# Attention denominators: a product with zeros and ones and one wide reciprocal in place of two block transpositions

## What is computed

```python
attn = softmax(scores, axis=-1)              # over the keys
ctx = einsum('bhqk,bhkd->bhqd', attn, v)     # [heads, tokens, 8]
ctx = ctx.transpose(0, 2, 1, 3).reshape(b, s, 128)
return ctx @ Wo
```

## Time and profile before

| | |
|---|---|
| median of 3 runs | 988.42 us (985.24 to 991.22) |
| the profiled execution's own time | 983.89 us |
| its span, first to last instruction | 982.1 us |
| mean granted TensorE clock | 0.953 of full speed |
| back stages | 32 (2 attentions, 16 items), first copy at 55.6 us, last at 838.8 us |

### The profile page before, as it was taken

The page is one execution under the profiler, slowest core; times in us unless marked ns, Lnnn a source line. Parts: engine busy times, 40 slices in busy tenths (PEclk is TensorE's granted clock), DMA queues, the critical chain, the costliest instruction groups (busy, mean ns, idle before and its releaser), DMA issues.

```text
span 982.1 us, 36375 instructions
## 1 busy us (share of the span) xinstructions
PE 846.8 (86%) x15235; PEld 514.6 (52%) x15235; DVE 641.8 (65%) x1566; ACT 557.4 (57%) x974; POOL 299.0 (30%) x387
## 2 busy tenths in 40 slices
PE   5888989889889988979887899798899789879895
PEld 3334435545444544545444545456465566757793
DVE  2547585976677566657767866568485566656773
ACT  3556747666485836745756566454558364425552
POOL 2432222222331322132223202325223343443452
PEclk9999999999799999979999899999999899989998
DMA  7998100000000000000000100001100011114633
GB/s 178 388 333 296 49 24 8 8 24 8 29 18 14 12 14 19 9 23 3 19 22 15 36 18 19 23 19 32 42 19 19 28 46 40 50 44 126 178 104 123
DMA packets 50190, 60.90 MB, mean 62 GB/s; under 512 B 5872, under 2 KB 36464, under 8 KB 49648
## 3 DMA queue, kind: packets, MB, share of 16 engines
q1 hardware_dynamic: 34768, 27.19, 9.6%
q10 hardware_dynamic: 10272, 21.14, 6.3%
q0 software_dynamic: 4992, 10.27, 3.1%
HBM read 22.92 MB, written 35.65 MB: 60 GB/s over the span
## 4 chain that ended last, share of the span: by engine, by line
PE 48%; DVE 27%; issue 11%; ACT 5%; POOL 4%; DMA 3%; another core or an unknown queue 1%; SPq 0%; POOLq 0%; DVEq 0%; ACTq 0%
DVE row_max L1336 13%; PE ps L927 9%; PE ps L787 6%; PE ps L754 5%; PE ps L1012 4%; PE ps L765 3%; POOL eo_rows L1640 2%; PE ps L801 2%; PE ps L810 2%; PE ps L1004 2%; PE ps L793 2%; PE ps L1006 2%; PE ps L1005 2%; ACT probs L1164 2%
## 5 line engine op out<-in xcount | busy, mean ns | idle before, releaser
L1336 DVE TENSOR_REDUCE row_max<-ps 128x4 f32<-128x1024 f32 (+1 forms) x256 | 267.7, 1078 | 109.6 <-PE ps L765 62.7
L1164 ACT ACTIVATE probs<-ps 128x1024 f32<-128x1024 f32 x128 | 130.1, 1029 | 77.8 <-PE ps L787 66.7
L754 PE MATMUL ps<-bias_t,ch 64*32 64x512 f16 x2048 | 112.1, 395 | 26.7 <-DVE row_max L1336 12.2
L1164 ACT ACTIVATE stage<-ps 128x1024 f32<-128x1024 f32 x96 | 96.9, 1025 | 60.1 <-remote 31.7
L1640 POOL DMA_INDIRECT eo_rows<-eo_t,to_t x92 | 89.4, 972 | 117.8 <-ACT eo_t L1216 97.0
L1604 POOL TENSOR_TENSOR ctx_sb<-ctx_raw,ctx_sb 128x512 f32<-128x512 f32 x32 | 40.7, 1272 | 172.6 <-DVE ctx_sb L1364 172.5
L927 PE MATMUL ps<-probs,v_pad 128*32 128x256 f32 x1024 | 85.4, 400 | 3.2 <-ACT probs L1164 2.0
L1004 PE MATMUL ps<-xT_t,wgu_hi 128*128 128x256 f16 x276 | 77.6, 281 | 8.8 <-issue 2.8
L1495 DVE SCALAR_TENSOR_TENSOR gate_s<-gate_t,ps 128x256 f32<-128x256 f32 x138 | 57.1, 414 | 40.5 <-ACT gate_t L1210 30.8
L1627 POOL DMA_INDIRECT slot_rows<-rows,slots x64 | 63.2, 987 | 66.1 <-DVE slots L1444 51.8
L1012 PE MATMUL ps<-wd,hid 128*128 x552 | 74.2, 287 | 9.9 <-ACT xT_t L1202 5.8
(11 more groups left out here) (168 smaller groups left out, 1596.1 us busy)
## 6 DMA issues: line engine op xcount, KB each, us to landing
slot_rows<-eo_g ACTq DMA_DIRECT2D x1, 12642.0 KB, 48.0
slot_rows<-eo_g ACTq DMA_DIRECT2D x1, 7998.0 KB, 26.1
x_t<-slot_rows SPq DMA_DIRECT2D x46, 129.0 KB
eo_g<-eo_rows SPq DMA_DIRECT2D x16, 256.0 KB
xT<-in_x SPq DMA_DIRECT2D x16, 128.0 KB
kept<-resid SPq DMA_DIRECT2D x16, 128.0 KB, 1.7
resid_b<-kept SPq DMA_DIRECT2D x16, 128.0 KB
out_dram<-outT SPq DMA_DIRECT2D x16, 128.0 KB
```

Of the source, the lines that this page charges most:

```text
L754: eng.matmul(ps[HR * c:HR * (c + 1), two[r], :].rearrange("p (j s) -> p j s", j=2), csth("flip")[half, :], bias_t[half, way, 2 * g:2 * g + ...
L1164: eng.activation(probs[a][:, 2 * (k % 2):2 * (k % 2) + 2, :], both_of("c%d" % a, i, "e%d" % k), ACT.Exp).then_inc(z["exp"], 1)
L1336: ins = eng.tensor_reduce(row_max[a][:, qt, 4 * g:4 * g + 4].rearrange("p (r j) -> p r j", r=2), of_heads, AX.X, ALU.max)
```

## The change

A 128x128 matrix of zeros and ones, `den`, joins the f32 constants (the late part of them, loaded to `cf` at L1672). Its column `m` has a single one, in the row that holds the denominator of the head to which row `m` belongs; rows 16 to 31 of a block, which hold no context, get a denominator as well. In place of the three VectorE steps, TensorE multiplies `den` with the whole of `ctx_raw` (one f32 product of 512 columns into a rotating bank, step `den`), so that every partition has its denominators in place, and VectorE takes one reciprocal of 128x512 from that bank to `ctx_sb` (step `rec`). The GpSimd product and the output product are as before. In the plan, `den` is given 0.85 us on TensorE and takes a bank, and `rec` 0.69 us on VectorE and gives it back. The wait for the late constants moves from the first `out` to the first `den`. The tiles `rden` and their two memsets go.

```diff
--- before.py
+++ after.py
@@ -41,7 +41,7 @@
 
 CF, CF_COLS = {}, 0
 for _n, _w in (("ident", P), ("centre", D), ("kmask", HJ), ("kones", HJ), ("expert", NX), ("tri", NX * NX), ("tile", T_MAX), ("eights", T_MAX),
-               ("first", len(PARTS) * NX), ("zero", 1), ("half", 1), ("own", 2), ("to", 2 * KT), ("cos", KT * HD), ("sin", KT * HD)):
+               ("first", len(PARTS) * NX), ("zero", 1), ("half", 1), ("own", 2), ("to", 2 * KT), ("cos", KT * HD), ("sin", KT * HD), ("den", P)):
     CF[_n] = (CF_COLS, CF_COLS + _w)
     CF_COLS += _w
 CH, CH_COLS = {}, 0
@@ -198,7 +198,7 @@
     def back(self, a, i, free):
         job = "b%d" % a
         last = self.op((job, i, "ctx"), "act", 0.60, [("c%d" % a, i, "end")] + self.before(job, i), (), X)
-        last = self.chain(job, i, last, ("byq", "dve", 0.62), ("rec", "dve", 0.35), ("byd", "dve", 0.62), ("ctxn", "pool", 1.3))
+        last = self.chain(job, i, last, ("den", "pe", 0.85, ONE), ("rec", "dve", 0.69, (), "mine"), ("ctxn", "pool", 1.3))
         return self.op((job, i, "out"), "pe", 0.88, [last] + free, ONE)
 
     def b1(self, i):
@@ -487,7 +487,7 @@
 
 
         q_rows, k_head, v_pad, probs = {}, {}, {}, {}
-        qk_tok, row_max, ctx_raw, ctx_sb, rden = {}, {}, {}, {}, {}
+        qk_tok, row_max, ctx_raw, ctx_sb = {}, {}, {}, {}
         for a in (1, 2):
             big = ("q_rows", 2 * NG * S, F16), ("k_head", 2 * NG * HJ * S, F16), \
                 ("v_pad", KT * H * HR, F32), ("probs", 4 * 2 * S, F32)
@@ -503,8 +503,6 @@
             row_max[a] = sb("row_max%d" % a, [P, KT, H])
             ctx_raw[a] = sb("ctx_raw%d" % a, [P, 2, S])
             ctx_sb[a] = sb("ctx_sb%d" % a, [P, 2, S])
-
-            rden[a] = sb("rden%d" % a, [P, KT * S // HR, 4])
         onehot = probs[1][0:NBUCKET, 0:2, :]
         by_parts = probs[1][0:H, 2:4, :].bitcast(F16).rearrange("h k (o f) -> h k o f", o=2)
 
@@ -630,7 +628,7 @@
                                                             ("r1", "sq var v root"), ("r2", "sq var v root spread n"))}
 
         att = {a: signals("a%d_" % a, "qk v hi again vz lo kspread qspread krow qrow score max "
-                          "mxhi mxlo maxt clear qmax wscore exp pv ctx byq rec byd ctxn o") for a in (1, 2)}
+                          "mxhi mxlo maxt clear qmax wscore exp pv ctx den rec ctxn o") for a in (1, 2)}
         x1_done, h2_done = sem("x1_done"), sem("h2_done")
         rot_done = signals("rot_", "cos sin sum")
         hand = signals("hand_", "tok hi lo to l step gap e hot both ahead rank slot resid")
@@ -684,6 +682,8 @@
                 return rot_done["sin"], i + 1
             if name == "out":
                 return (x1_done if job == "b1" else h2_done), i + 1
+            if name == "den":
+                return z["rec"], i + 1
             if name in ("centre", "turn"):
                 return norm["n" + job[1]]["n" if name == "centre" else "h"], i + 1
             return {"qk": z["lo"], "v": z["vz"], "c0": z["ctx"], 
@@ -932,10 +932,14 @@
 
         def pe_back(eng, a, i, at):
             job, z = "b%d" % a, att[a]
+            yield at("den")
+            bank = free_bank(eng, job, i, "den")
+            if a == 1 and i == 0:
+                eng.wait_ge(s_w2, 16 * N_W2)
+            eng.wait_ge(z["ctx"], i + 1)
+            eng.matmul(bank, cst("den"), ctx_raw[a][:, :, :].rearrange("p r s -> p (r s)"), start=True, stop=True).then_inc(z["den"], 1)
             yield at("out")
             bank = free_bank(eng, job, i, "out")
-            if a == 1 and i == 0:
-                eng.wait_ge(s_w2, 16 * N_W2)
             eng.wait_ge(z["ctxn"], i + 1)
             eng.matmul(bank[:, 0:S], W["o%da" % a], ctx_sb[a][:, 0, :], start=True, stop=False)
             eng.matmul(bank[:, 0:S], W["o%db" % a], ctx_sb[a][:, 1, :], start=False, stop=True).then_inc(z["o"], 1)
@@ -1350,20 +1354,11 @@
 
         def dve_back(eng, a, i, at):
             z, job = att[a], "b%d" % a
-            yield at("byq")
-            eng.wait_ge(z["ctx"], i + 1)
+            yield at("rec")
+            eng.wait_ge(z["den"], i + 1)
             if i:
                 eng.wait_ge(z["o"], i)
-            flat = ctx_sb[a][:, :, :].rearrange("p r s -> p (r s)")
-            eng.transpose(flat, ctx_raw[a][:, :, :].rearrange("p r s -> p (r s)")).then_inc(z["byq"], 1)
-            yield at("rec")
-            eng.wait_ge(z["byq"], i + 1)
-            eng.reciprocal(rden[a][:, :, 0:2], flat.rearrange("p (n m) -> p n m", m=HR)[:, :, 16:18]).then_inc(z["rec"], 1)
-            yield at("byd")
-            eng.wait_ge(z["rec"], i + 1)
-            eng.transpose(flat.rearrange("p (n d) -> p n d", d=HD),
-                          rden[a][:, :, :].rearrange("p n k -> p (n k)").unsqueeze(2).to_broadcast([P, 4 * KT * S // HR, HD])) \
-               .then_inc(z["byd"], 1)
+            eng.reciprocal(ctx_sb[a][:, :, :], held(job, i, "den").rearrange("p (r s) -> p r s", r=2)).then_inc(z["rec"], 1)
 
         def dve_b1(eng, i):
             z, at = att[1], due("b1", i)
@@ -1547,8 +1542,6 @@
         def pool_setup(eng):
             eng.memset(ones_d[:, :], 1.0 / D)
             eng.memset(ones_h[:, :], 1.0)
-            for a in (1, 2):
-                eng.memset(rden[a][:, :, :], 0.0)
             eng.memset(blank, 0.0).then_inc(su["filled"], 1)
             for g, (first, _) in enumerate(PARTS):
                 eng.memset(ahead[:, first + g, :], 0.0)
@@ -1600,7 +1593,7 @@
         def pool_context(eng, a, i):
 
             yield PLACE["b%d" % a, i, "ctxn"]
-            eng.wait_ge(att[a]["byd"], i + 1)
+            eng.wait_ge(att[a]["rec"], i + 1)
             eng.tensor_tensor(ctx_sb[a][:, :, :], ctx_raw[a][:, :, :], ctx_sb[a][:, :, :], ALU.mult).then_inc(att[a]["ctxn"], 1)
 
         def pool_b2(eng, i):
@@ -1789,6 +1782,11 @@
     p, n = np.arange(P)[:, None], np.arange(P)[None, :]
     put("ident", np.eye(P))
     put("centre", np.eye(D) - 1.0 / D)
+
+    den = np.zeros((P, P))
+    for m in range(P):
+        den[m // HR * HR + 2 * HD + (1 if HD <= m % HR < 2 * HD else 0), m] = 1.0
+    put("den", den)
     inv = 1.0 / 10000.0 ** (np.arange(0, HD, 2, dtype=np.float32) / HD)
     freq = np.einsum("i,j->ij", np.arange(S, dtype=np.float32), inv)
     emb = np.concatenate([freq, freq], axis=-1).T
```

## The result

The changed kernel takes 1082.16 us (median of 4 runs, 1076.54 to 1082.67) where the kernel before, on the same chip, takes 986.93: a ratio of 1.0945, with a 95% interval of 1.0892 to 1.0997. That is 95 us more for +42 forecast, outside the range (up to 1066) and beyond every rival (up to 1067). The sign was right, the size was not.

A forecast was written before the change was run, and what follows sets the result against it. It took a chain alternating between TensorE (86% busy) and VectorE (65%) as the bound. Reciprocal 49.8 less 25.9 removed is +23.9 us, product +18.1: +42.0 on the profiled 983.9, plus 4.5 to the median, 1030 us; range 1003 to 1055, with rivals 1066.

The forecast's parts named there:

- +42: Whole kernel: net loss forecast, +23.9 us on VectorE plus +18.1 us on TensorE, giving 1030 us, 4.2% slower.
- every rival: Three: ordinary reciprocal, 973.0 or 991.1 us (chance 0.14); nothing hides, 1062 (0.15); price above the slope, 1067 (0.12).
- The reciprocal's price: VectorE's new 128x512 reciprocal: 3.11 us each from the slope of two smaller reciprocals, 99.5 us busy over 32.
- the share of 0.50: Part of the new reciprocal's 99.5 busy us on VectorE taken to lie on the chain: 49.8 us.
- Rival 2: VectorE and TensorE: nothing of the added time hides, 43.7 + 30.1 = 73.8 us, so 1062 us; chance 0.15.
- The product: TensorE's new f32 product for each context: 0.94 us each, 30.1 us over 32, of which +18.1 us reach the end.
- The share of 0.60: Part of the new product's 30.1 us on TensorE that reaches the end, set between 56 and 65%.
- The saving: VectorE's two transpositions and small reciprocal removed: 55.9 us busy, 25.9 us of it on the chain.
- At nothing: Effects priced at zero: longer way from context copy to GpSimd product, the product's bank (0 to 21 us), late constants' wait.
- The thin cover of the output product: Output product waited only 1.2 us for GpSimd, so little hides the context's extra 1 us or more; left to the shares.

The follow-up runs named there:

- e2: Changed kernel in its own order, wide reciprocal replaced by a tensor_scalar (times 1/256) of the same 128x512, denominators not inverted: 988.89 us, ratio 0.9974.
- e1: Changed kernel with only the planner's figure for the wide reciprocal set from 0.69 to its measured 3.35 us: 1028.08 us, ratio 1.0388.
- e5: Changed kernel with the reciprocal cut into four of 128x128, each planned at 0.92 us: 1031.2 us, ratio 1.0413.
- e12: Kernel before plus one unread 128x256 reciprocal in each back stage, known to the planner (2.3 us for the step, not 0.62): 1027.27 us, ratio 1.0326.
- e3: Kernel before, in its own order, plus one unread 128x256 reciprocal in each back stage, unknown to the planner: 1038.76 us, ratio 1.0468.
- e11: Changed kernel, plan still 0.69 us, with the reciprocal on half of the columns and a tensor_scalar on the other half: 1030.36 us, ratio 1.0338.
- e13: Changed kernel with 3.35 us planned for the reciprocal and BUSY at 0.2, so 36 warm-up matmuls for 177: 1039.8 us, ratio 1.0477.
- e4: Kernel before with only the new f32 product added, planned at 0.85 us and with a bank, its result unread: 988.68 us, ratio 0.9988.
- e9: Changed kernel with the reciprocal taken by ScalarE as exponential of the negative logarithm, two operations planned at 0.6 us each: 1020.69 us, ratio 1.0293.

## Why the prediction was wrong, point by point

1. **The reciprocal's price** (3.11 us) was low by 0.24 us, 7.7 us busy over 32. The slope between the two small rows, 5.77 ns an element, is 6.3 between 256 and 512 elements ((3351 - 1737) / 256). Taking rows of the same operation was right, and so was not believing the 0.69 of the plan. The Trainium skill (VectorE: DVE Perf Modes, section First, the fixed hardware budget) gives the reciprocal's divide step a repeat count of 8. Read as 8 clocks an element at the 0.96 GHz of the same page (Specifications), that is an estimated 8.3 ns; the rows show 6.3 ns, about six such clocks.
2. **The step that failed is the share of 0.50.** I saw that the planner "puts the next DVE work 2.4 us too early" and priced this with 0.50 for 0.48, that is at next to nothing. The share is about right for work that the plan knows: between e2 and e1 lie 41 us for 85 us busy, 0.48 (e5 gives 0.46, e12 0.58). For the same work unknown to the plan it is 96 for 85, 1.12 (e3 gives 0.83, e11 0.79). What the runs showed in place of my share is thus 1.12, and the missing term is 55 us, the difference between the change and e1. My +42 us is close to e1's +38: I forecast the kernel with a right plan.
3. **Rival 2 named the mechanism but capped it wrongly.** It supposed that at worst each added us costs one, 1062 us. Measured is more. The first 1.43 us cost 36 us in all and the next 1.24 cost 60. A stall of TensorE is not only its own length: the granted clock falls from 0.942 (e11) to 0.926, and TensorE's busy time rises from 880.1 to 897.2 us for the same instructions, against 60 us of time. By e13 only a part of such an increase reaches the end: there the matmuls other than warm-ups are busy some 28 us longer than in e1, for about 9 us of time. Where the rest of the excess comes from, beyond waits that follow on waits, stays open.
4. **The product** was forecast at +18.1 and costs nothing (e4: 0.9988, with 1.0022 at the upper end, 2 us). The share of 0.60, taken between PE's mean and the output product, doesn't carry over. The planner drops 35 warm-ups in its favour and the clock is higher; that the new product also stands early in its stage, and not at the end where others wait for it, is my reading and was not tested.
5. **The saving.** I took the three steps off at 25.9 us. No run removes them with nothing in their place. The nearest is e2, where 21.9 us busy stand for their 55.9: at the shares of my sum that is 25.9 less 10.9, a gain of 15 us, and it measured 2.6 (6 to -1). Why the rest is missing stays open: VectorE's busy time as a whole fell by 12 us only, which at 0.46 would be 5 us, so this does not show that a share misprices a removal. Points 4 and 5 nearly cancel (+18.1 and -15 forecast, together -2.6 measured in e2). That the sum still met e1 is luck in part.
6. **At nothing**: rightly so for the bank and the constants (e4 has both). The thin cover of the output product was real: its wait for GpSimd went from 1.2 to 10.0 us, and in e3 the same wait is 15.4; with the true cost in the plan (e1) it is 1.5.

## What to carry to other kernels

Where the order of all engines is fixed ahead from assumed durations, a duration that is wrong by a factor of five can cost more than the time itself (96 us for 85 here): give the planner the measured figure first, and judge the change then. Cost an operation from rows of that operation at two sizes; a reciprocal on VectorE is some five times as dear per element as a tensor_scalar here (6.3 ns for (684 - 359) / 256 = 1.27), so count how often each value is inverted, not how many instructions there are. A share of the chain priced added work roughly right where the order knew of it (0.46 to 0.58 measured for 0.50); for work that the order did not know it was too low (0.79 to 1.12).

## What the runs showed of the hardware

- VectorE's reciprocal, f32: 166 ns for 2 elements a partition, 339 for 32, 935 for 128, 1737 for 256, 3351 for 512; from 128 on 6.3 ns an element, whether it reads PSUM or SBUF. A tensor_scalar of 512 took 684 ns.
- ScalarE reloads its tables between logarithm and exponential, at 1.283 us each time, 64 times in e9 beyond the one load that every kernel has. Tanh, exponential and copies needed none between them.
- A f32 product of 512 columns added for every context, 35.0 us of records in e4, cost nothing measurable on a TensorE that was 86% busy; 35 warm-up matmuls fell away, and the granted clock was higher (0.957 to 0.967 over ten runs, for 0.941 to 0.955).
- The granted clock falls with unplanned waits of TensorE: 0.965 in e2 and 0.926 in the changed kernel, same instructions on TensorE and same order. Between e1 and e13 (0.967 and 0.934) lie about 9 us.
